# Joining the first batch's heads inside the second batch's attention, with root and transposes, in a two-layer hybrid kernel

## The reference, cut to what matters

```python
h = _rms(x, n1_w)
q, k, v = _rms(heads(wq), qn_w), _rms(heads(wk), kn_w), heads(wv)   # 16 heads of 8
scores = where(causal, einsum('bhqd,bhkd->bhqk', q, k) * HD ** -0.5, -inf)
ao = softmax(scores) @ v, heads joined, @ wo.T         # projection
x1 = x + ao
h2 = _rms(x1, n2_w)
probs = softmax(h2 @ gate_w.T)                         # router, the best 2 of 4 experts
e0 = gelu(h2 @ e0_up.T) @ e0_down.T
e1 = (silu(h2 @ e1_w1.T) * (h2 @ e1_w2.T)) @ e1_down.T
e2, e3 = longer chains of gelu layers
out = x1 + sum over the chosen experts of weight * expert(h2)
```

## Time and profile before

| | |
|---|---|
| median of 3 runs | 1145.88 us (1145.13 to 1147.95) |
| the profiled execution's own time | 1146.39 us |
| its span, first to last instruction | 1144.6 us |
| TensorE busy | 671.8 us, 59% |
| VectorE busy | 828.1 us, 72% |
| ScalarE busy | 531.2 us, 46% |
| GpSimd busy | 327.0 us, 29% |
| mean granted TensorE clock | 0.78 of full |

### The profile page before, as it was taken

The page is one execution under the profiler, slowest core; times in us unless marked ns, Lnnn a source line. Parts: engine busy times, 40 slices in busy tenths (PEclk is TensorE's granted clock), DMA queues, the critical chain, the costliest instruction groups (busy, mean ns, idle before and its releaser), DMA issues.

```text
span 1144.6 us, 11976 instructions
## 1 busy us (share of the span) xinstructions
PE 671.8 (59%) x4000; PEld 325.1 (28%) x4000; DVE 828.1 (72%) x1478; ACT 531.2 (46%) x880; POOL 327.0 (29%) x290
## 2 busy tenths in 40 slices
PE   3993004000004106598887899872275988878997
PEld 1452004000003104222223555520251222235655
DVE  5799999888889998966566722369979575677212
ACT  2414003333331005699996332253056999963331
POOL 1060652000003303256664000007802567640000
PEclk9995555555555558599999899987575999998999
DMA  3150048500000010541110000000006311100001
GB/s 96 56 157 8 3 96 180 137 19 19 0 19 19 0 20 17 180 128 57 38 48 1 1 1 1 1 1 0 0 1 206 101 57 45 41 1 0 1 1 38
DMA packets 37206, 51.30 MB, mean 45 GB/s; under 512 B 5081, under 2 KB 26969, under 8 KB 36121
## 3 DMA queue, kind: packets, MB, share of 16 engines
q1 hardware_dynamic: 36376, 49.75, 15.7%
q10 hardware_dynamic: 768, 0.79, 0.4%
HBM read 21.02 MB, written 16.92 MB: 33 GB/s over the span
## 4 chain that ended last, share of the span: by engine, by line
DVE 45%; PE 23%; POOL 12%; ACT 8%; issue 8%; DMA 2%; SPq 1%; ACTq 1%; POOLq 0%; DVEq 0%
POOL PX L1283 11%; PE PS L1404 6%; ACT PX L1523 5%; PE PS L1382 5%; PE PS L1424 4%; DVE D L843 4%; DVE S L847 4%; DVE P L844 3%; DVE P L840 3%; DVE mag L1075 2%; DVE RP L862 2%; DVE PRR L861 2%; PE PS L1363 1%; DVE CUM L1090 1%; DVE PS L907 1%
## 5 line engine op out<-in xcount | busy, mean ns | idle before, releaser
L1523 ACT ACTIVATE PX<-PS 128x1024 f32<-128x1024 f32 (+1 forms) x320 | 270.1, 986 | 10.8 <-PE PS L1345 10.8
L1283 POOL TENSOR_TENSOR PX<-PX,maskf 128x256 f32<-128x256 f32 (+1 forms) x192 | 177.0, 955 | 115.9 <-ACT PX L1523 115.7
L1363 PE MATMUL PS<-PX,VA 128*32 128x512 f32 (+3 forms) x1536 | 166.6, 504 | 27.5 <-POOL PX L1283 18.6
L1730 DVE SCALAR_TENSOR_TENSOR X<-PS,wts,X 128x96 f32<-128x96 f32 x128 | 38.4, 315 | 118.2 <-PE PS L1424 103.9
L1345 PE MATMUL PS<-QS,KS 64*128 64x512 bf16 (+3 forms) x768 | 106.3, 338 | 7.8 <-ACT PX L1523 4.4
L1667 DVE RECIPROCAL DEN<-DEN 128x512 f32<-128x512 f32 x32 | 107.3, 3353 | 1.1
L611 PE MATMUL PS<-fw,ones 128*128 128x384 f32 x2 | 1.6, 926 | 160.0 <-DVE fw L1547 160.0
L718 ACT ACTIVATE P<-S,AC 128x16 f32<-128x16 f32 x128 | 41.2, 322 | 114.4 <-DVE S L847 114.4
L983 POOL TENSOR_TENSOR PRQ<-PA,LQK 128x2048 f32<-128x2048 f32 (+7 forms) x8 | 20.8, 2606 | 200.4 <-DMA WS<-S 183.1
L1382 PE MATMUL PS<-HT,fw 128*128 128x512 f32 x144 | 71.0, 636 | 4.0 <-DVE HG L1697 2.6
L1665 DVE LOAD_MASK_SELECT DEN<-PS x32 | 0.4, 14 | 98.3 <-PE PS L1363 96.8
(11 more groups left out here) (276 smaller groups left out, 1488.6 us busy)
## 6 DMA issues: line engine op xcount, KB each, us to landing
QS<-qs_d SPq DMA_DIRECT2D x64, 98.0 KB
qs_d<-QP SPq DMA_DIRECT2D x24, 256.0 KB, 3.6
ks_d<-QP SPq DMA_DIRECT2D x24, 256.0 KB, 3.9
KS<-ks_d SPq DMA_DIRECT2D x64, 96.0 KB
K<-LQK SPq DMA_DIRECT2D x16, 256.0 KB
W<-WS SPq DMA_DIRECT2D x16, 256.0 KB, 4.4
qkv_d<-CY SPq DMA_DIRECT2D x3, 1024.0 KB, 4.0
LQK<-qkv_d SPq DMA_DIRECT2D x8, 256.0 KB, 4.6
```

What stands on the lines that cost most here:

```text
L1283: pool.tensor_tensor(block, block, bcast(maskf[:], 1, 2 * halves), ALU.mult).then_inc(probs_masked, 1)
L1363: last = pe.matmul(PS[32 * h:32 * h + 32, SCORES_BANKS + qc, c0:CH], VA[b][:, kt, h, :], px[:, i % 2, at:at + CH - c0], start=(kt == 0), s ...
L1523: act.activation(tile(PX[u % PDEPTH][:]), tile(PS[:, k:k + 2, :]), ACT.Exp).then_inc(probs_ready, 1)
```

## The change

A first part of the join moves into the attention of the second batch. At unit 17 of iterations 4 and 5, behind the values' product of unit 13, TensorE projects chunk 0 or 1 into bank 6, once VectorE has read that bank; at the same place of iterations 6 and 7 it transposes chunk 0 or 1 into bank 6. VectorE, after the first half of the iteration, adds the chunk (iterations 4 and 5), squares and sums (5), normalises (6), and copies the transposed chunk to `HT` itself (6 and 7; ScalarE did this before). ScalarE takes the first batch's root after unit 6 of iteration 6. Bank 6 is then used for both, and TensorE waits for its reading before the next iteration's values.

After the attention, up 0 a goes first, then the second batch's projections (banks 4 and 5), up 0 b, up 1 a and b, down 0, the second batch's transposes, down 1, router, up 2, up 3, down 2. ScalarE does SiLU 0 and 1 ahead of the second root; VectorE does gate 1 ahead of the routing, gate 2 within it (behind its first comparison) and gate 3 behind the first expert adds; gates 2 and 3 wait for the down that reads their buffer. The residual sum goes behind gate 1. The output is stored in four pieces of 256 KB, each once its chunk is complete. The operations are the same, but for the two copies that change engine.

```diff
+        JOIN_AT = 17
@@ f_tensor, within the values' product of a unit
                     if kt == 0:
                         pe.wait_ge(o_read, (rep * B * NG + it) * 2 + qc + 1)
+                        if qc == 0 and it in (NG + 1, NG + 2):
+                            pe.wait_ge(proj_added, rep * NCH + it - NG)
+                        if qc == 0 and it == NG + 3:
+                            banks.all_read()
...
                     last.then_inc(probs_used, units)
+                if u < NA and u % NA_B == JOIN_AT and u // NA_B >= NG:
+                    it = u // NA_B
+                    pe.wait_ge(heads_added, (rep * B + 1) * (NG - 1) * 2)
+                    pe.wait_ge(o_read, OBANKS + (rep * B * NG + it) * 2 + 1)
+                    if it < NG + 2:
+                        proj(it - NG, SCORES_BANKS)
+                    else:
+                        c = it - NG - 2
+                        pe.wait_ge(normed, FIRST_NORM[nth] * B + 1)
+                        pe_transpose_in(pe, banks, SQ, FIRST_NORM[nth], range(c, c + 1), SCORES_BANKS - c)
@@ f_tensor, after the attention
+            banks.all_read()
+            up(0, 0, F_E1A)
+            pe.wait_ge(heads_added, (rep * B + 2) * (NG - 1) * 2)
+            for c in range(NCH // B, NCH):
+                proj(c, HT_BANKS + c - NCH // B)
+            up(0, 2, F_E1B)
+            pe.wait_ge(up_read, hidden + 1)
+            up(1, 0, F_E1A)
+            pe.wait_ge(h1_ready, gated + 1)
+            up(1, 2, F_E1B)
+            down1(0)
+            pe_transpose_in(pe, banks, SQ, FIRST_NORM[nth], range(NCH // B, NCH), HT_BANKS - NCH // B)
+            down1(1)
+            banks.all_read()
...
+            for c in range(NCH // B, NCH):
+                pe.wait_ge(up_read, hidden + c)
+                up(c, 0, F_E1A)
+                pe.wait_ge(h1_ready, gated + c)
+                up(c, 2, F_E1B)
+            down1(NCH - 2)
@@ f_scalar
                 act.activation(tile(PX[u % PDEPTH][:]), tile(PS[:, k:k + 2, :]), ACT.Exp).then_inc(probs_ready, 1)
+                if u == (NG + 2) * NA_B + NA_Q0:
+                    act_sqrt(act, ask, stat[:, 0:TB])
...
+            silu(0)
+            silu(1)
+            act_sqrt(act, ask, stat[:, TB:2 * TB])
+            act_ht(act, reads, range(NCH // B, NCH), HT_BANKS - NCH // B)
+            reads.n += 1
+            ask.wait()
+            act.activation(pr[:], lg[:], ACT.Exp).then_inc(to_dve, 1)
+            silu(2)
+            silu(3)
@@ f_vector, after each half of an iteration
+                    if qc == 0 and it in (NG, NG + 1):
+                        join(it - NG, SCORES_BANKS)
+                    if qc == 0 and it == NG + 1:
+                        join_squares(0)
+                    if qc == 0 and it == NG + 2:
+                        join_normed(0)
+                    if qc == 0 and it >= NG + 2:
+                        c = it - NG - 2
+                        v.wait_ge(psum_full, base + NCH + TILES + 4 * NCH + c + 1)
+                        v.tensor_copy(HT[:, c * CH:(c + 1) * CH], PS[:, SCORES_BANKS, :]).then_inc(psum_read, 1)
@@ f_vector, after the attention
+            for c in range(NCH // B, NCH):
+                join(c, HT_BANKS + c - NCH // B)
+            join_squares(1)
...
             gate(0)
+            join_normed(1)
+            gate(1)
+            v.tensor_tensor(X[:], X[:], XL[:], ALU.add).then_inc(x_sum, 1)
...
             for i in range(E4):
+                if i == 2:
+                    gate(2)
...
+            add1(0)
+            gate(3)
             for c in range(1, NCH):
-                gate(c)
-                add1(c - 1)
-            add1(NCH - 1)
+                add1(c)
@@ the store
-            sp.wait_ge(x_ready, len(LAYERS))
-            sp.dma_start(out.rearrange("(t p) d -> p t d", p=P), X[:]).then_inc(out_stored, 16)
-            sp.wait_ge(out_stored, 16)
+            for c in range(NCH):
+                ts = slice(c * TPC, (c + 1) * TPC)
+                sp.wait_ge(down_read, 3 * TILES + (c + 1) * TPC)
+                sp.dma_start(out.rearrange("(t p) d -> p t d", p=P)[:, ts], X[:, ts]).then_inc(out_stored, 16)
+            sp.wait_ge(out_stored, 16 * NCH)
```

More of the change, by code:

```diff
@@ L1327, in f_tensor, with proj @@
             banks.all_read()
+            def proj(c, bank):
+                for i in range(TPC):
+                    t = (c * TPC + i) * P
+                    last = pe.matmul(PS[:, bank, i * OUTC:(i + 1) * OUTC], AO[:, t:t + P], fwo[:], start=True, stop=True)
+                last.then_inc(proj_full, 1)
             for u in range(NA + LAG):
@@ L1384, in up @@
                 last.then_inc(up_full, 1)
[L1386 to L1395, removed]
             hidden = rep * UPS
@@ L1426, in down @@
                     last.then_inc(down_full, 1)
[L1429 to L1435, removed]
+            banks.all_read()
[12 more added lines that the diff above has]
+            banks.all_read()
+            banks.n += 1
+            for t in range(TILES):
+                last = pe.matmul(PS[:, ROUTER_BANK, t * E4:(t + 1) * E4], HT[:, t * P:(t + 1) * P],
+                                 fw[:, F_GATE:F_GATE + E4], start=True, stop=True)
+            last.then_inc(psum_full, 1)
+            assert banks.n == base + F_RES
+            for c in range(NCH // B, NCH):
[4 more added lines that the diff above has]
+            down1(NCH - 2)
             pe.wait_ge(up_read, hidden + NCH)
@@ L1523, in f_scalar, with silu @@
                 act.activation(tile(PX[u % PDEPTH][:]), tile(PS[:, k:k + 2, :]), ACT.Exp).then_inc(probs_ready, 1)
[L1524 to L1526 removed]
+                if u == (NG + 2) * NA_B + NA_Q0:
+                    act_sqrt(act, ask, stat[:, 0:TB])
             hidden = rep * 8 * NCH
[L1528 to L1532 removed]
+            def silu(c):
                 act.wait_ge(up_full, hidden + 2 * c + 1)
@@ L1651, in f_vector, with join, join_squares, join_normed @@
             link.close()
+            def join(c, bank):
+                v.wait_ge(proj_full, rep * NCH + c + 1)
+                t = slice(c * TPC, (c + 1) * TPC)
+                v.tensor_tensor(XL[:, t, KEEP:], XL[:, t, KEEP:],
+                                PS[:, bank, 0:TPC * OUTC].rearrange("p (t d) -> p t d", d=OUTC),
+                                ALU.add).then_inc(proj_added, 1)
+            def join_squares(b):
+                tb = slice(b * TB, (b + 1) * TB)
+                v.wait_ge(proj_added, rep * NCH + NCH // B * (b + 1))
+                link(v.tensor_tensor(SQ[:, tb], XL[:, tb], XL[:, tb], ALU.mult))
+                link(v.tensor_reduce(stat[:, tb], SQ[:, tb], AX.X, ALU.add))
+                v.tensor_scalar(stat[:, tb], stat[:, tb], 1.0 / D, F_EPS, ALU.mult, ALU.add).then_inc(to_act, 1)
+            def join_normed(b):
+                tb = slice(b * TB, (b + 1) * TB)
+                ans.wait()
+                link(v.reciprocal(rrms[:, tb], stat[:, tb]))
+                v.tensor_tensor(SQ[:, tb], XL[:, tb], bcast(rrms[:, tb], 2, D), ALU.mult).then_inc(normed, 1)
             added = 2 * (NG - 1) * B * rep
```

33 lines of the change are left out of this document (3 added, 30 removed).

## The result

The change makes the kernel slower by half a per cent. Its median is 1152.06 us (1149.85 to 1155.54, 7 runs), against 1146.97 us (1145.13 to 1147.95, 7 runs) for the kernel before, run beside it: a ratio of 1.0052, 95% interval 1.004 to 1.0063, or 5 to 6 us. (The ratio is taken over the runs; the quotient of the two medians alone would be 1.0044.) The profiled execution took 1154.43 us with a span of 1152.6.

What follows compares the result with a forecast made beforehand. ScalarE's exponentials and GpSimd's masks were taken to bound the attention, a chain through all engines the join. Attention +9.2, join -7.2 and output -1.5 gave +0.5 us, forecast 1146.4 us, range 1138.0 to 1154.8.

Steps and rivals of the forecast that it cites:

- TensorE at half clock throughout the join: Rival, chance 0.15: TensorE stays at half clock behind the attention, ups hold gate 0, SiLU 1 and root; +8.9, 1154.8 us.
- a drain at each switch: Rival, chance 0.07: each of four mid-stream ScalarE table switches costs another 1.28 us; 5.1 in all, 1151.5 us.
- TensorE waiting at four places: Rival, chance 0.05: TensorE's new waits stand for VectorE, each of four places a layer costing another 1 us; 1154.4 us.
- Part 1: ScalarE root with two table loads in iteration 6 of the attention: +2.7 us a layer, bounds 0 and 2.9.
- a fall of the clock inside the attention: Sign that the prediction is wrong: TensorE's clock falls inside the attention; no size given.
- Parts 2 and 3: Attention iterations 4 and 5: two projections on TensorE, +0.65 us each; VectorE squares beside GpSimd masks, +0.2 us.
- Part 4: Two transposes on TensorE in attention iterations 6 and 7: +0.2 us each, 0.4 a layer, bounds 0 and 1.1.
- Part 5: Attention's end to second expert phase: 38.3 us a layer, gaining 4.5 and 2.7, 7.2 us in all.
- The term for the clock: Behind the router and around the 4.2 us gap: 0.8 of one 1.7 us half-clock loss, 1.4 us a layer.
- The full clock rival: Rival, chance 0.26: the join behind the attention runs at full clock, gaining 13.8 us; -6.1 in all, 1139.8 us.
- Part 6: Residual sum on VectorE moved behind gate 1, ending ahead of the router: 0 us.
- Part 7: Output in four pieces at the kernel's end: last 256 KB lands in 3.6 us, -1.5 us, bounds 0 and -3.8.

Runs made afterwards that it cites:

- attn_only: Kernel before with only the changed attention; behind it the old order and one store: 1154.31 us, ratio 1.007 to the kernel before.
- gate2_late: Kernel after with gate 2 moved from within the routing to just ahead of the first expert adds: 1147.41 us, ratio 1.0003 to the kernel before.
- out4: Kernel before with only the output store split into four pieces of 256 KB: 1144.56 us, ratio 0.9977 to the kernel before.
- root_after: Kernel after with the first batch's root, scaling and transposes moved behind the attention, ScalarE copying: 1144.51 us, ratio 0.998 to the kernel before.
- no_root: Kernel after without the first batch's square root and its two table loads, so scaled wrongly: 1152.4 us in one execution.
- combo: Kernel after with the edits of root_after and gate2_late together: 1135.92 us, ratio 0.9919 to the kernel before.
- combo2: combo with up 0 b ahead of the heads' wait, gates 0 and 1 earlier, router ahead of down 1: 1134.92 us, ratio 0.989 to the kernel before.

## Why the prediction was off, point by point

The forecast was +0.5 us; the medians say +5.1. The 1152.1 us measured lie within the wide range of 1138.0 to 1154.8, but outside the forecast's own 1142.6 to 1149.2, and the outcome, slower by more than 3.4 us, had been given 0.27. That it is inside is owed to the width: the range was opened on that side for three rivals, TensorE at half clock throughout the join, a drain at each switch and TensorE waiting at four places, and none of them is what happened. After's clock was back at full 11.5 and 10.6 us behind T in the two layers. The drain's 1151.5 us is near by chance. By the steps:

- **Part 1, root inside the attention:** the mechanism held, and its size as far as ScalarE goes (2.94 us for 2.9 forecast; no drain, so that rival falls). What was missing is what ScalarE's pause does to TensorE. Parts 1 and 4 put 2.9 us on iteration 6; it grew by 3.8 and 3.5. The prediction named a fall of the clock inside the attention as what would make it wrong, and gave it no term: the second step that failed. In all 6 layers looked at with the root inside (after, attn_only, gate2_late) the clock fell to half for 3.4 us in iteration 6, and it fell there in none of the 12 of before, out4, root_after, no_root, combo and combo2. Of the missing 0.6 to 0.9 us some 0.2 are not the switch's (see parts 2 and 3); that the rest is this stretch is an inference: no kernel had the switch without the fall.
- **Parts 2 and 3, projections and squares:** 0.72 and 0.60 us for 0.65 and 0.85. The forecast's own figures (scores done at 582.5, exponential at 583.0) give a cover of 0.5 us and not the 0.35 it used; 0.65 came nearer than the 0.5 that would follow. The cost is the mask of unit 18 that waits for its exponential, in after's timeline of GpSimd:

```profile
586.60 1.61 POOL L1284 TENSOR_TENSOR PX<-PX,maskf 128x512 f32<-128x512 f32 x1 [0.61 <-ACT PX L1542]
```

  The 0.2 for squares beside masks did not show in iteration 5, but it was there: this mask overlaps the squares and took 1.61 us, where the same mask of iteration 4 took 1.29, and it ends in iteration 6. That one takes 17.53 us in root_after, which has neither root nor transposes in it, against 17.34 before: 0.2, as forecast, one iteration later. **Part 4** in iteration 7: 0.03 for 0.2. The attention as a whole: 10.0 for 9.2.
- **Part 5, the join: the step that failed.** 7.2 us were to come back, 4.5 and 2.7; up to the second phase 2.4 and 0.7 did, 3.1 in all. The order, the waits and even the 4.2 us ahead of down 2 were right. The term for the clock was mis-sized: 1.4 us a layer for all of it. Measured against the steps at full clock: the router ends 0.8 us later than forecast in the first layer and 0.3 us earlier in the second; gate 2 starts 5.4 us behind the router instead of 3.7, 1.7 more in both (658.26 - 652.82; 1060.82 - 1055.38); down 2 takes 2.67 and 3.70 us of the chain instead of 1.76, 0.9 and 1.9 more. With 0.1 a layer of small pieces that is 3.5 + 3.4 us, less the 2.8 that the forecast had put there: 4.1 of lost gain. The full clock rival (a gain of 13.8 in the two layers together) is nowhere near. The sizes by layer are of one execution each; that gate 2 starts 5.4 us behind the router shows in both layers of after and root_after alike. And of the 3.1 us another part goes behind the boundary that I had chosen, since the half clock reaches into the second phase: T to the first GELU product is 47.3 and 46.8 us against 48.7 and 46.9, 1.5 in all (1.4 with T read alike).
- **Why a slow up is so dear there:** before, half clock behind the router in the second layer cost nothing visible, since VectorE ended the routing without it. The change put gate 2 into the routing and so tied VectorE's longest chain to TensorE's slowest stretch. Undoing that tie alone gave 5.6 us with the root inside (gate2_late) and 7.0 with the root behind (combo against root_after).
- **Part 6:** the residual sum lies ahead of the router's end, 0, as forecast.
- **Part 7, output:** 2.8 us for 1.5 (5.5 us from last issue to the end of the span before, 2.7 after; 2.6 by out4's ratio). The nearest row, stores of 256 KB at 3.6 us, was of transfers issued several at a time; a single one lands in 2.3. The prediction's estimate after the Trainium skill, "DMA: Bandwidth & Descriptors", a gain of 2.3, was nearer than my own term, and still short; the page (Anatomy of one DMA) gives its fixed part of about 2.0 us for DMAs issued by GpSimd, and these are issued by SyncE.

The balance by stages is 10.0 - 1.5 - 2.8 = +5.7 us, beside +5.1 by the medians. Against the forecast's +0.5 that is 5.2 us: 0.8 more from the attention and 4.1 less gained in the join up to the second phase, with 1.6 lost behind it, less 1.3 that the store gave more than expected.

One thing was not weighed at all: the prediction asked what the root costs inside the attention and never what it costs where it had been. root_after answers: nothing, because the first batch's root and transposes fit in the 3.8 us in which TensorE waits for the last heads anyway.

## What to carry to other kernels

Price a moved step at both places: work that fits into an idle gap which stays there anyway is already free, and moving it into a full pipeline can only cost. On an engine with a long serial chain, place a wait by the latest time at which its input can come, here with TensorE at half clock behind a gap or a router, not by the time at full clock. And look at what else the stalled pipeline feeds: a pause of 2.9 us on ScalarE emptied TensorE and was followed by half clock.

## What the runs showed of the hardware

- TensorE's granted clock fell to 0.50 for 3.4 us behind the table switch, in 6 of 6 layers; in after's first layer TensorE had been busy 1.33 of the 3.6 us ahead of it. With one idle gap of 1.31 us in the same iteration (no_root) it stayed at 1.00.
- It also fell behind the router in both layers (from 653.2 and 1056.0 on), though the records show TensorE busy through the 3.66 us of 4-column matmuls. In the ten kernels profiled the clock fell between the router's start, less 0.1 us, and 0.9 us behind its end in 18 of 20 layers. The other two, the first of the kernel before and the second of out4, had been at half clock until 1.6 us ahead of the router and did not fall. What in the router is followed by that, its narrow matmuls or the idle time shortly ahead of it (0.45 us in front of the transposes in after), was not tried and stays open.
- Small VectorE operations beside GpSimd's masks took 0.65 to 1.21 us instead of 0.17, one of 1024 columns 2.27 instead of 1.22, in step with masks of 0.73 and 1.28 us. In after, the scale of the sums (8 columns) took 1.11 us beside a mask and 0.17 in the join.
- A lone store of 256 KB landed 2.3 us after its issue (2.5 in one of 8), one of 1024 KB 5.1.
